# A decoder kernel on one NeuronCore: the causal mask of the attention scores as one 512-column product per PSUM bank

## The reference, cut to what matters

```python
scores = jnp.einsum('bhqd,bhkd->bhqk', q, k) * SCALE
causal = jnp.tril(jnp.ones((s, s), dtype=bool))
scores = jnp.where(causal[None, None], scores, -jnp.inf)
probs = jax.nn.softmax(scores, axis=-1)
ctx = jnp.einsum('bhqk,bhkd->bhqd', probs, v)
...
return jnp.einsum('bsd,ed->bse', ctx, w_proj) + b_proj
```

## Time and profile before

| What | Value |
|---|---|
| Runs of the kernel before | 822.9, 822.99, 824.99 us |
| The profiled execution, its own time | 823.1 us |
| Its span, first to last instruction | 821.3 us |
| Busy: PE, DVE, POOL, ACT | 745.7, 642.5, 482.3, 397.8 us |
| Mean granted TensorE clock | 0.97 of full speed |
| L197 (mask products) | 128 rows, mean 279 ns each |
| L200 (score products) | 256 rows, mean 426 ns each |

### The profile page before, as it was taken

One profiled execution on the slowest core, in us unless ns is written; L12 is line 12 of the kernel. 1 busy time (PEld: TensorE's weight loads), 2 busy tenths in 40 slices (PEclk: granted clock), 3 DMA queues, 4 the chain that ended last, 5 costly groups with the idle time before them and its releaser, 6 DMA issues. The chain is left out here.

```text
span 821.3 us, 13489 instructions
## 1 busy us (share of the span) xinstructions
PE 745.7 (91%) x4390; PEld 510.2 (62%) x4414; DVE 642.5 (78%) x1291; ACT 397.8 (48%) x641; POOL 482.3 (59%) x721
## 2 busy tenths in 40 slices
PE   6999999998999599999869999989899669999895
PEld 5677777764444277777647777765444337777674
DVE  3667777757999777774849999978999779988874
ACT  1555555553304344443676778860100036777785
POOL 1112333447776344441256777799878379899993
PEclk9999999999999799999989999989999969999998
DMA  7900000001100500000030221103000000000001
GB/s 272 363 2 2 1 2 2 1 2 73 80 1 0 196 1 1 1 2 1 0 132 37 67 70 61 51 2 119 1 0 0 1 0 1 1 20 14 14 21 39
DMA packets 12868, 33.97 MB, mean 41 GB/s; under 512 B 2688, under 2 KB 8064, under 8 KB 11520
## 3 DMA queue, kind: packets, MB, share of 16 engines
q1 hardware_dynamic: 12800, 33.11, 11.2%
HBM read 30.94 MB, written 2.16 MB: 40 GB/s over the span
## 5 line engine op out<-in xcount | busy, mean ns | idle before, releaser
L1081 PE MATMUL bank<-XT,win_late 128*128 128x256 f32 x320 | 87.9, 402 | 4.5 <-DVE ss_xc L1331 4.3
L467 POOL TENSOR_TENSOR at_kbd<-at_qk,at_hmask 128x512 f32<-128x512 f32 x16 | 16.6, 1040 | 113.5 <-DVE at_qk L394 113.5
L639 DVE TENSOR_REDUCE MIX<-m_pr 128x128 f32<-128x1024 f32 x64 | 77.3, 1211 | 0.4
L587 POOL TENSOR_TENSOR m_kv<-XT,CTXT 128x512 f32<-128x512 f32 x64 | 67.5, 1076 | 9.7 <-PE bank L612 9.7
L587 POOL TENSOR_TENSOR m_kv<-CTXT 128x512 f32<-128x512 f32 x64 | 65.0, 1038 | 12.2 <-PE bank L612 12.2
L1331 DVE SCALAR_TENSOR_TENSOR ss_xc<-bank,cw_late,ss_xc 128x254 f32<-128x254 f32 x144 | 66.5, 476 | 4.0 <-ACT ss_xc L1204 0.5
L1081 PEld LDWEIGHTS bank<-XT,win_late 128*128 128x128 f32 x320 | 56.9, 195 | 19.6 <-DVE ss_xc L1331 12.5
L610 PE MATMUL bank<-m_kv,toep 128*128 128x512 f32 x128 | 65.9, 596 | 2.8 <-POOL m_kv L587 2.8
L612 PE MATMUL bank<-m_kv,toep 128*128 128x512 f32 x128 | 65.4, 592 | 0.0
L611 PE MATMUL bank<-m_kv,toep 128*128 128x512 f32 x128 | 65.4, 592 | 0.0
L1634 PE MATMUL bank<-had_last,f_ht 128*128 128x256 f32 x256 | 61.8, 386 | 0.0
(11 more groups left out here) (233 smaller groups left out, 1893.8 us busy)
## 6 DMA issues: line engine op xcount, KB each, us to landing
MIX<-cum_rows SPq DMA_DIRECT2D x16, 512.0 KB, 3.7
toep<-toep_dram SPq DMA_DIRECT2D x2, 2048.0 KB, 11.5
X<-x_dram SPq DMA_DIRECT2D x1, 2048.0 KB, 12.2
CTXT<-ctxT_dram SPq DMA_DIRECT2D x1, 2048.0 KB, 17.6
out_dram<-f_o SPq DMA_DIRECT2D x16, 128.0 KB, 1.7
XT<-xT_dram SPq DMA_DIRECT2D x1, 1280.0 KB, 7.9
win_late<-win_dram SPq DMA_DIRECT2D x1, 1280.0 KB, 5.2
wgu<-wgu_dram SPq DMA_DIRECT2D x1, 1024.0 KB, 5.2
```

Source lines behind the costliest of these rows:

```text
L587: m = nc.gpsimd.tensor_tensor(KV[n % 3][:, c, :, :].rearrange("p (b j) i -> p b j i", b=HB), ki, vj, ALU.mult)
L639: nc.vector.tensor_reduce(head(MIX)[:, :, a, bass.ts(h, HB), :], PR[n % 2][:, :, :, :].rearrange("p c (b j) i -> p c b j i", b=HB), op=ALU ...
L1081: m = nc.tensor.matmul(bX[(NU * g + n) % 3][:, 0:GS_], win[:, h, off:off + P], XT[:, h, bass.ts(g, GS_)], start=(h == 0), stop=(h == C - 1))
```

## The change

The bf16 mask tile is twice as wide (4 x 128 columns, the mask four times). PE puts it on each bank with one product of 512 columns, four in all per sequence, ahead of both groups of scores; then come the g = 0 and g = 1 products back to back, the last of them closing the accumulation. ScalarE casts the mask with two instructions in place of one. `maskf` is no tile of its own any more but lies in CN[0].

```diff
--- before.py
+++ after.py
@@ -105,8 +105,7 @@
     bp = ch.sb("at_bp", [P, D])
     bp2 = ch.sb("at_bpv", [P, D])
     hmask = ch.sb("at_hmask", [P, 2])
-    mask = ch.sb("at_mask", [P, 2, S], BF16)
-    maskf = ch.sb("at_maskf", [P, 2, S])
+    mask = ch.sb("at_mask", [P, 4, S], BF16)
     QK = [ch.sb(f"at_qk{k}", [P, 4, S]) for k in range(3)]
     VP = [ch.sb(f"at_v{k}", [P, H0, 32]) for k in range(4)]
     KBD = [ch.sb(f"at_kbd{k}", [P, 2, 2, S]) for k in range(2)]
@@ -114,6 +113,7 @@
     PTs = [ch.sb(f"at_pt{k}", [P, H0, S]) for k in range(2)]
     CTs = [ch.sb(f"at_ct{k}", [P, 4, S]) for k in range(2)]
     CN = [ch.sb(f"at_cn{k}", [P, D]) for k in range(2)]
+    maskf = CN[0][:, :].rearrange("p (a s) -> p a s", a=2)
     CNT = [ch.sb(f"at_cnt{k}", [P, C, S]) for k in range(2)]
     XR = [ch.sb(f"at_xr{k}", [P, D]) for k in range(2)]
     Y = [ch.sb(f"at_y{k}", [P, D]) for k in range(3)]
@@ -192,12 +192,12 @@
                 pe.wait_ge(s["consts"], 2)
             pe.wait_ge(s["k_spread"], n + 1)
             upto(pe, s["shifted"], 4 * n)
+            for t in range(4):
+                nc.tensor.matmul(bS[t][:, :], identb[:, :], mask[:, :, :], start=True, stop=False)
             for g in range(2):
                 for t in range(4):
-                    nc.tensor.matmul(bS[t][:, bass.ts(g, 2 * S)], identb[:, :], mask[:, :, :], start=True, stop=False)
-                for t in range(4):
                     rows = slice(RT * t, RT * t + RT)
-                    m = nc.tensor.matmul(bS[t][:, bass.ts(g, 2 * S)], QK[n % 3][rows, g, :], KBD[n % 2][rows, g, :, :], start=False, stop=True)
+                    m = nc.tensor.matmul(bS[t][:, bass.ts(g, 2 * S)], QK[n % 3][rows, g, :], KBD[n % 2][rows, g, :, :], start=False, stop=(g == 1))
                     if g:
                         m.then_inc(s["scored"], 1)
 
@@ -307,7 +307,9 @@
     def scalar(act):
         act.wait_ge(s["value_in"], 48)
         nc.scalar.copy(identb[:, :], ident[:, :])
-        nc.scalar.copy(mask[:, :, :], maskf[:, :, :]).then_inc(s["consts"], 1)
+        for g in range(2):
+            m = nc.scalar.copy(mask[:, bass.ts(g, 2), :], maskf[:, :, :])
+        m.then_inc(s["consts"], 1)
 
         def keep_p(n, t):
             if not 0 <= n < B:
```

## The result

| | before | after |
|---|---|---|
| Runs in one comparison, us | 821.35, 822.83, 822.9, 822.99, 824.99 | 817.31, 817.4, 818.92, 818.99, 819.53 |
| Median | 822.9 | 818.92 |
| Profiled execution / its span | 823.1 / 821.3 | 819.53 / 817.7 |
| Start of the last sequence's masks in the trace | 162.86 | 157.73 |

The time falls by 0.57%: ratio 0.9943, 95% interval 0.992 to 0.9965.

A forecast was written before the change was run, and what follows sets the result against it. PE was taken as the bound, 91% busy overall and without waits in the attention step; 15 sequences x 0.33 us + 0.25 us for the first = 5.2 us off 823.1 gave 817.9 us, range 815.6 to 821.4.

The forecast's parts named there:

- (a): Masks in `score`: eight 256-column products become four of 512, one border term goes, 0.11 us saved per sequence.
- (b): Scores: two groups of 8 product instructions become one stretch of 16, one entry-and-exit goes, 0.21 us saved per sequence.
- rival 1: The borders within the scores stay, so only the mask saving remains: 821.1 us; chance 10%.
- rival 3: Second score group's products run one after another on banks still being written: 838 us, at half the price 828; chance 3%.
- rival 4: A 512-column mask product costs more than two of 256; with 0.03 us more each, 819.8 us; chance 3%.
- (c): First sequence, partly at the 1.2 GHz clock: masks cost about 1.44 us as now, 0.25 us saved in all.
- (d): ScalarE's second mask cast at the start: 0.40 us more, covered because PE reaches its first mask over 5 us later.
- (e): `maskf` placed in CN[0]: same transfer to another place, CN[0] first written four steps later; costs nothing.
- (f): All masks ahead of the g = 0 products: nobody reads a bank before `scored`, which comes sooner; nothing added.
- The sum: Whole kernel: 15 sequences x 0.33 + 0.25 = 5.2 us off the profiled execution's 823.1 us, giving 817.9 us.
- so the rest moves forward as a whole: Behind the attention nothing waits for a fixed point in time, so the whole saving reaches the end.
- Rival 2: Part of the gain is given back in longer half-rate clock stretches: loss of 3 us, 820.9 us; chance 7%.

The follow-up runs named there:

- e1: The changed kernel with the mask put on in eight products of 256 columns, all ahead of both score groups; ratio to the kernel before 0.9958.
- e2: The changed kernel with the output projection moved between the g = 0 and g = 1 scores; ratio to the kernel before 1.0048.
- e3: The changed kernel with the four context products of a step in two adjoining pairs instead of four single groups; ratio to the kernel before 0.9905.
- e6: e3 with VectorE's residual addition ahead of its first peak of the step; ratio to the kernel before 0.9882.
- e8: e3 with the value projection ahead of the first-quarter transposes on PE, ScalarE's copies swapped alike; ratio to the kernel before 0.9883.

## Why the prediction was right, and where it was off

- **What bounds the kernel.** PE, with no wait at the mask from the third sequence on: right. The step fell by 0.33 us for 0.33 us taken out of `score`.
- **(a) Masks**, 1.08 to 0.97: measured 0.97. **(b) Scores**, 1.29 to 1.08: measured 1.08. The context products were a good stand-in for row groups; rival 1 (821.1) and rival 3 (828 to 838) are out, and two groups on the same four row groups stream at 0.215 us a round, 4 x 0.215 of the 1.08. The Trainium skill, "TensorE: Matmul & The Clock Gate", section "The mechanism" (the prediction names the section that follows it), says that a weight load overlaps only a matmul of another row group, though it also lets a load go ahead that targets the background weight buffer. With the first of these alone each round would have waited for its loads, and the trace disagrees; no row tells which buffer they went to. e1 shows that (a) too is a border and not a width, as the sum had it; rival 4 is out. (Rival 1 was priced at 0.12 a sequence where (a) has 0.11, which would make it 821.3 and not 821.1; nothing hangs on it.)
- **(c) The first sequence**: 0.25 predicted, 0.33 measured. The masks, forecast to stay at 1.44, took 1.33 (13.79 to 15.12): the sum had let the half rate last for all of the 0.90 us of the first mask group, its border included. The 0.33 that was named for a sooner rise is what came.
- **(d), (e), (f) at nothing**: PE's first mask started right behind L173 as before, and DVE's wait pattern is unchanged.
- **The sum** in the attention was 5.2; the trace has 5.26 (5.46 less the 0.20 of an earlier start). The profiled execution came out 3.57 shorter in all. The term that was mis-sized is the one I set at zero under "so the rest moves forward as a whole": behind the attention 1.5 us net went at the half-rate stretch at 188 us, and 0.3 net in the blocks behind, where I have not followed them up. Rival 2 had that mechanism, but placed it at 420 and 640 us and not at the first wait behind the attention, which stands in the earlier trace rows with its 2.23 us. The rest of that block did move as a whole. The ratio over all runs, 4.7 us of 822.9, lies between the profiled execution's 3.57 and the forecast.
- **Luck.** The profiled spans are 821.3, 821.8 and 820.7 before and 817.7 and 817.9 after, 2.8 to 4.1 apart; no pair keeps the whole 5.2 to the end. The 5.26 in the attention was no luck. That the median came within 1 us of the forecast was in part: the sum had nothing for what is given back behind the attention, and how much that is differs from execution to execution.

## What to carry to other kernels

Where a TensorE stream is the bound, count the borders at which the division of the array changes (full, row groups, column groups), not the instructions: each exit and each entry into f32 full-array work costs about 0.1 us here (the 0.99, 1.09 and 1.88 us of L173), and adjoining groups of one kind chain without a border (1.08 us for two score groups). Before moving an instruction to save a border, list who waits for its result or its bank, since it may be the cover of another wait (e2, e3, e6, e8). And a saving of 0.6% on a kernel whose identical executions differ by 0.4% (five runs) to 0.7% (nineteen runs, 820.16 to 825.98 us) has to be read from the step in the trace first and from the end time second.

## What the runs showed of the hardware that I had not expected

- The full-rate clock came early or late in the same program: sixteen L173 instructions take 2.02 us in one execution and 3.76 in two others of the kernel before.
- The same 2.23 us wait is followed by full rate in one execution and by products of 2.05 and 1.84 us instead of 1.02 in another.
- Joining one context group of 32 columns to the next saves 0.33 us, of which the groups' own start-to-start distances show only 0.13: the other 0.20 is on the full-array work before and behind it.
